# Cross attention over 2048 context rows: heads side by side in row groups of the matrix engine

## What is computed

```python
q = (Q @ Wq.T + bq).reshape(m, -1, H, HD)      # l1x; l2x has no biases on q, k, v and no mask
k = (K @ Wk.T + bk).reshape(m, -1, H, HD)
v = (V @ Wv.T + bv).reshape(m, -1, H, HD)
energy = jnp.einsum('mqhd,mkhd->mhqk', q, k) * SCALE
energy = jnp.where(mask == 0, jnp.float32(-1e+20), energy)
out = jnp.einsum('mhqk,mkhd->mqhd', softmax(energy, axis=3), v)
```

## Time and profile before

| what | before |
|---|---|
| time, median of 3 runs | 623.72 us (621.22 to 623.9) |
| the profiled execution | 620.94 us, span 619.1 us |
| busy: TensorE / its weight loads | 496.6 us (80%) / 379.5 us (61%) |
| busy: DVE / ACT / POOL | 346.1 / 233.6 / 54.0 us |
| chain that ended last | PE 58%, DVE 26%, ACT 7%, issue 4%, DMA 3% |
| mean granted TensorE clock | 0.891 |
| DMA | 42.97 MB, mean 69 GB/s |

### The profile page before, as it was taken

The page is one execution under the profiler, slowest core; times in us unless marked ns, Lnnn a source line. Parts: engine busy times, 40 slices in busy tenths (PEclk is TensorE's granted clock), DMA queues, the critical chain, the costliest instruction groups (busy, mean ns, idle before and its releaser), DMA issues.

```text
span 619.1 us, 9252 instructions
## 1 busy us (share of the span) xinstructions
PE 496.6 (80%) x3712; PEld 379.5 (61%) x3712; DVE 346.1 (56%) x790; ACT 233.6 (38%) x452; POOL 54.0 (9%) x116
## 2 busy tenths in 40 slices
PE   6788659999658706899977677778999999878686
PEld 4656556444538606444446567767888888777685
DVE  5464458771569324867434654346777666643533
ACT  7013305778014202056723314235555555501031
POOL 0400020000022011100021021200000000000000
PEclk9777959999978958599998986989999999987899
DMA  8628100000619784400020000000000000045000
GB/s 292 283 52 167 57 0 1 1 2 2 257 52 371 157 199 178 170 0 1 2 103 1 1 1 1 1 1 1 1 0 1 1 2 1 0 170 238 1 1 5
DMA packets 8005, 42.97 MB, mean 69 GB/s; under 512 B 1050, under 2 KB 4122, under 8 KB 4762
## 3 DMA queue, kind: packets, MB, share of 16 engines
q1 hardware_dynamic: 6811, 33.71, 16.7%
q0 software_dynamic: 1152, 8.68, 3.9%
HBM read 35.69 MB, written 0.08 MB: 58 GB/s over the span
## 4 chain that ended last, share of the span: by engine, by line
PE 58%; DVE 26%; ACT 7%; issue 4%; DMA 3%; POOL 1%; SPq 0%; POOLq 0%; DVEq 0%; ACTq 0%
PE banks L260 53%; PE banks L263 5%; DVE small L2150 3%; ACT probs L2225 3%; DVE peaks L1373 3%; DVE weights_lo L2160 2%; DMA region<-in_tree_f,leaf_no 2%; DVE xn L346 1%; DVE sbq L1609 1%; POOL mv L352 1%; ACT weights_hi L2238 1%; DMA ctxT<-in_ctxT 1%; DVE tB L1889 1%; DVE xnT L365 1%; DVE st L342 1%
## 5 line engine op out<-in xcount | busy, mean ns | idle before, releaser
L1373 DVE TENSOR_REDUCE peaks<-banks 128x1 f32<-128x1024 f32 x64 | 76.7, 1221 | 16.2 <-PE banks L260 16.0
L260 PE MATMUL banks<-identb 128*128 128x128 bf16 x637 | 48.1, 234 | 23.3 <-DMA region<-in_tree_f,leaf_no 15.0
L263 PE MATMUL banks<-p_first,probs 128*128 128x128 f32 x320 | 51.9, 300 | 14.9 <-ACT probs L618 5.1
L260 PEld LDWEIGHTS banks<-identb 128*128 128x128 bf16 x637 | 43.4, 106 | 26.6 <-DMA region<-in_tree_f,leaf_no 15.7
L2238 ACT CAST weights_hi<-banks 128x512 fp32r<-128x512 f32 x64 | 36.0, 588 | 53.8 <-PE banks L263 53.8
L263 PEld LDWEIGHTS banks<-p_first,probs 128*128 128x128 f32 x320 | 40.1, 153 | 26.0 <-ACT probs L618 6.4
L2150 DVE TENSOR_REDUCE small<-banks 128x1 f32<-128x1024 f32 x32 | 39.0, 1218 | 26.8 <-PE banks L260 26.8
L2160 DVE TENSOR_TENSOR weights_lo<-banks,weights_hi 128x512 fp32r<-128x512 f32 x64 | 41.6, 682 | 13.1 <-ACT weights_hi L2238 13.1
L1434 ACT ACTIVATE probs<-banks 128x512 f32<-128x512 f32 x64 | 34.8, 596 | 32.8 <-PE banks L260 31.8
L1434 ACT ACTIVATE probs<-banks,seen 128x512 f32<-128x512 f32 x64 | 40.2, 686 | 11.8 <-PE banks L260 11.8
L260 PE MATMUL banks<-probs,values 128*32 128x256 f32 x512 | 41.7, 395 | 0.5 <-DVE keysT L1394 0.5
(11 more groups left out here) (435 smaller groups left out, 903.2 us busy)
## 6 DMA issues: line engine op xcount, KB each, us to landing
region<-in_w_l2f SPq DMA_DIRECT2D x1, 4096.0 KB, 12.8
region<-in_w_l3f SPq DMA_DIRECT2D x1, 4096.0 KB, 12.0
region<-in_w_b SPq DMA_DIRECT2D x1, 3076.0 KB, 10.3
values<-in_ctx SPq DMA_DIRECT2D x2, 1024.0 KB, 7.7
region<-in_w_l0f SPq DMA_DIRECT2D x1, 2048.0 KB, 21.6
keys_l1x<-shared SPq DMA_DIRECT2D x8, 256.0 KB, 4.0
keys_l2x<-probsT SPq DMA_DIRECT2D x8, 256.0 KB
region<-in_w_l3d SPq DMA_DIRECT2D x1, 2048.0 KB, 15.6
```

The source lines that it names most:

```text
L260: return nc.tensor.matmul(o, lhsT, rhs, start=start, stop=stop)
L263: return nc.tensor.transpose(o, i, ident[0:n, 0:n])
L1373: nc.vector.tensor_reduce(peaks[:, h // 4 % 2, i:i + 1], ps[:, 2 * a:2 * a + 2, :], AX.XY, ALU.max, negate=True).then_inc(VM.sem, VM.now(( ...
```

## The change

- Each head of a quad gets a row group of 32: 8 rows of high, 8 of high, 8 of remainder, then three rows for mask and shift (`ROWS_OF` = 27). The query is `packed`: 128 columns per quad, no spreading.
- `peak(k)` now does one context bank for two heads: two matmuls of 512 columns in neighbouring row groups. DVE reduces 128x1024 to two columns, and a reduce over the four banks follows.
- `scores(u)` does two units (two heads, the same four context tiles): eight matmuls of 27 rows with 128 columns, alternating between two row groups. `weigh(w, half)` waits for the exps of all four heads.
- The query is made in two parts, quad 0 first; the weights' columns are regrouped by ACT copies (`regroup`), the bias comes in by a matmul, the mask's sign as a scale.
- l2x's keys are projected in l1x's lead-in, between its peaks (`early`), copied by ACT twice; POOL makes the remainders; SP stacks them right then. l2x's values move behind l1f's last node product. l2x's lead-in gets `keep(9, 7)` per peak, and the trees of k and v lose their `keep`.
- Stacking takes 48 DMAs of 64 KB per stage. The rows for mask and shift come by four more DMAs. The `w_l0f` load is issued after the mask row.
- The k tree's leaf lies in `probs` and `values_t`.

The core of the diff:

```diff
-            sp.wait_ge(V.sem, V.at((tag, "low", 3)))
+            low = G if tag == "l2x" else V
+            sp.wait_ge(low.sem, low.at((tag, "low", 3)))
+            if tag == "l2x":
+                for g in range(4):
+                    r = slice(32 * g + 24, 32 * g + ROWS_OF)
+                    load("rows_l2x", keys_r["l2x"][r, :, :].bitcast(F32), keys_r["l1x"][r, :, :].bitcast(F32))
             for t in range(4):
                 for part in range(3):
-                    src = (high if part < 2 else keysT[:, :])[32 * t:32 * t + 32, :]
-                    load("keys_" + tag, keys_r[tag][32 * part:32 * part + 32, t, :].bitcast(F32), src)
-                if tag == "l1x" and t:
-                    load("keys_" + tag, keys_r[tag][96:97, t, :].bitcast(F32), keys_r[tag][96:97, 0, :].bitcast(F32))
...
+                    src = high if part < 2 else keysT[:, :]
+                    for g in range(4):
+                        row = 32 * g + 8 * part
+                        load(f"keys_{tag}{t}", keys_r[tag][row:row + 8, t, :].bitcast(F32).rearrange("p (a b) -> p a b", a=2),
+                             src[32 * t + 8 * g:32 * t + 8 * g + 8, :].rearrange("p (a b) -> p a b", a=2))
...
+            sp.wait_ge(V.sem, V.at("mask.row"))
+            sp.wait_ge(A.sem, A.at(("shown", 3)))
+            for g in range(4):
+                load("rows_l1x", keys_r["l1x"][32 * g + 24:32 * g + 25, :, :].bitcast(F32),
+                     bc(keysT[96:97, :], 1, [1, 4, CTX]))
...
             stack_keys(sp, "l1x", shared[:, :])
-            loaded(sp, "keys_l1x")
+            loaded(sp, "keys_l1x3")
             load("node", nodew, dram["node"])
             load("node", nbias, dram["nbias"].partition_broadcast(P))
+            stack_keys(sp, "l2x", wide_high)
+            loaded(sp, "rows_l2x")
             sp.wait_ge(V.sem, V.at("l1x.o"))
             load("w_b", region[:, w_b_at:w_b_at + width(W_B)], dram["w_b"])
             load("w_c", region[:, w_b_at + width(W_B):2 * REG], dram["w_c"])
-            sp.wait_ge(T.sem, T.at(("o", "k")))
-            stack_keys(sp, "l2x", wide_high)
...
+        def key_scalar(act, b):
+
+            act.wait_ge(T.sem, T.at(("l2x", "kp", b)))
+            c = slice(b * BANK, (b + 1) * BANK)
+            nc.scalar.copy(wide_high[:, c].bitcast(F32R), ps[:, KEY_BANKS[b], :])
+            nc.scalar.copy(keysT[:, c], ps[:, KEY_BANKS[b], :]).then_inc(A.sem, A.now(("l2x", "k", b)))
+
+        def low_gpsimd(pool, b):
+
+            pool.wait_ge(A.sem, A.at(("l2x", "k", b)))
+            c = slice(b * BANK, (b + 1) * BANK)
+            nc.gpsimd.tensor_tensor(keysT[:, c], keysT[:, c], wide_high[:, c], ALU.subtract).then_inc(
+                G.sem, G.now(("l2x", "low", b)))
...
+                pe.wait_ge(A.sem, A.at(tag + ".wq"))
                 pe.wait_ge(V.sem, V.at(tag + ".xn.T"))
                 for t in range(4):
-                    m = mm(ps[:, 4, t * P:(t + 1) * P], w("q")[:, t * P:(t + 1) * P], xnT[:, :])
-                m.then_inc(T.sem, T.now(tag + ".q"))
-                loaded(pe, "keys_" + tag)
+                    o = ps[:, 5 if t else 4, t * P:(t + 1) * P]
+                    m = mm(o, at["w_l0x"][:, t * P:(t + 1) * P], xnT[:, :], True, not masked)
+                    if masked:
+                        m = mm(o, bias_rows[:, :], ident[0:4, t:t + 1].broadcast_to([4, P]), False, True)
+                    if t in (0, 3):
+                        m.then_inc(T.sem, T.now((tag + ".q", t // 3)))
...
-                    for b in (2 * a, 2 * a + 1):
-                        m = mm(ps[:, b, :], query_r[0:SHOWN, h * P:(h + 1) * P],
-                               keys[0:SHOWN, h // 4, b * BANK:(b + 1) * BANK])
-                    m.then_inc(PS.sem, PS.now((tag, h, a)))
...
+                    for g in (2 * a, 2 * a + 1):
+                        m = mm(ps[:, g, :], packed[group(g), q * P:(q + 1) * P],
+                               keys[group(g), q, c * BANK:(c + 1) * BANK])
+                    m.then_inc(PS.sem, PS.now((tag, k)))
 
...
-                def score(u):
-
-                    q, t = u // UNITS, u % UNITS
-                    if t == 0:
+                def scores(u):
+
+                    q, c = u // UNITS, u % UNITS // 4
+                    if u % UNITS == 0:
                         pe.wait_ge(VQ.sem, VQ.at((tag, q)))
...
-                    mm(ps[:, 4 + u % 3, :], keys[0:SHOWN, q, t * P:(t + 1) * P],
-                       query_r[0:SHOWN, 4 * q * P:4 * (q + 1) * P]).then_inc(PU.sem, PU.now((tag, u)))
-
-                def weigh(u):
-
-                    q, t = u // UNITS, u % UNITS
-                    if t == 0 and q:
+                    for j in range(4):
+                        t = 4 * c + j
+                        for i in range(2):
+                            g = (u + i) % 4
+                            if j == 0 and u + i >= 3:
+                                pe.wait_ge(AP_.sem, AP_.at((tag, u + i - 3)))
+                            m = mm(ps[:, 4 + (u + i) % 3, j * P:(j + 1) * P], keys[group(g), q, t * P:(t + 1) * P],
+                                   packed[group(g), q * P:(q + 1) * P])
+                            if j == 3:
+                                m.then_inc(PU.sem, PU.now((tag, u + i)))
+
+                def weigh(w, half):
+
+                    q, c = w // 4, w % 4
+                    if c == 0 and q and not half:
                         pe.wait_ge(VO.sem, VO.at((tag, q - 1)))
-                    pe.wait_ge(AP_.sem, AP_.at((tag, u)))
-                    for i in range(2):
-                        j = 2 * (t % 2) + i
-                        v = t * VW + (2 * q + i) * PW
-                        m = mm(ps[32 * j:32 * j + 32, 7, 0:2 * P], values_t[:, v:v + 32],
-                               probs[:, u % 8 // 4, u % 4 * BANK + i * 2 * P:u % 4 * BANK + (i + 1) * 2 * P],
-                               t < 2, t >= KT_N - 2)
-                    m.then_inc(PV.sem, PV.now((tag, u)))
+                    pe.wait_ge(AP_.sem, AP_.at((tag, 4 * w + 3)))
+                    of = probs[:, w % 2, :].rearrange("p (g j n) -> p g j n", g=4, j=4)
+                    for j in (2 * half, 2 * half + 1):
+                        t = 4 * c + j
+                        for i in range(2):
+                            r = 32 * (2 * (t % 2) + i)
+                            v = t * VW + (2 * q + i) * PW
+                            m = mm(ps[r:r + 32, 7, 0:2 * P].rearrange("p (h n) -> p h n", h=2), values_t[:, v:v + 32],
+                                   of[:, 2 * i:2 * i + 2, j, :], t < 2, t >= KT_N - 2)
...
+                early = {0: (key, 0), 1: (value, 0), 2: (value, 1), 3: (key, 1), 4: (key, 2), 5: (value, 2), 6: (key, 3),
+                         7: (value, 3)}
                 for k in range(9):
                     peak(k)
-                    if masked and k:
-                        value(2 * k - 2)
-                        value(2 * k - 1)
+                    if masked and k < 8:
+                        step, b = early[k]
+                        step(b)
+                    elif not masked and k:
+                        keep(9, 7)
                 if masked:
                     pe.wait_ge(A.sem, A.at((tag, "v", 3)))
                 turn(0)
                 peak(9)
-                score(0)
-                score(1)
+                scores(0)
                 peak(10)
                 for v in range(last // 2):
                     q, c = v // 8, v % 8
                     if v < last // 2 - 1:
-                        score(2 * v + 2)
-                        score(2 * v + 3)
+                        scores(2 * v + 2)
                     if c == 6 and q + 1 < QUADS:
                         turn(q + 1)
                     peak(v + LEAD)
-                    weigh(2 * v)
-                    weigh(2 * v + 1)
+                    if v:
+                        weigh((v - 1) // 2, (v - 1) % 2)
                     if v == last // 2 - 2:
-                        pe.wait_ge(VM.sem, VM.at((tag, H - 1, 1)))
+                        pe.wait_ge(VM.sem, VM.at((tag, PEAKS - 1)))
                         for i in range(QUADS - 1):
                             fold(i)
+                weigh(last // 4 - 1, 1)
...
-                loaded(dve, "keys_" + tag)
-                nc.vector.memset(hi[96:128, :], 1.0 if masked else 0.0).then_inc(V.sem, V.now(tag + ".ones"))
...
-                spread(nc.vector, 0).then_inc(V.sem, V.now((tag, "q", 0)))
...
+                for i in range(2):
+                    dve.wait_ge(A.sem, A.at((tag + ".qhi", i)))
+                    o = packed[:, thirds[i]]
+                    nc.vector.scalar_tensor_tensor(o, product(i), sign[:, 0:1], o.bitcast(F32), ALU.mult,
+                                                   ALU.add).then_inc(V.sem, V.now((tag + ".qs", i)))
...
+                    o = packed[:, q * P:(q + 1) * P]
```

(19 more changed lines are left out.)

277 lines of the change are left out of this document (155 added, 122 removed).

## The result

The changed kernel takes 670.93 us (median of 4 runs, 668.33 to 674.88) against 623.55 us before (4 runs on the same chip): a ratio of 1.077, 95% interval 1.071 to 1.084. The forecast was 604 us, so it fell on the wrong side, by more than any rival allowed. The profiled execution of the changed kernel took 669.75 us (span 667.8).

A forecast was written before the change was run, and what follows sets the result against it. TensorE was taken to bound the cross loops' turns. Savings of 3.0 (loops), 3.0 (l2x start), 3.3 (l1x start), 3.0 (trees) and 4.8 (last gather) made 17.1 us off 620.94: 603.8, rounded to 604, range 588 to 624.

The forecast's parts named there:

- Part 1: Peaks in row groups: two 512-column matmuls in different groups overlap, so a pair costs 0.22 us rather than 0.44.
- Part 2: Scores in row groups: eight 128-column matmuls per turn, 256 loads in a stage instead of 64, taken at 0.47 us.
- S: Time of one turn's scores in the cross loops: 0.47 us, outer bounds 0.25 and 0.93.
- Part 3: The cross loops' turn: 1.49 us against 1.68; with the losses counted, 1.5 us saved per stage, 3.0 for both.
- 0.23 left over and 0.57 weighing, which stay: In a loop turn, array-shape changes and waits (0.23 us) and weighing (0.57) were kept at their old length.
- short fp32r matmuls run at fp32's pace: Rival, chance 0.13: fp32r scores of 128 columns take four passes per column, 0.88 us; turn 1.90, kernel 630.0.
- TensorE stays the bound by 0.1: In loop turns with peaks, TensorE's 1.49 us stays above VectorE's own pace of 1.38.
- late turns: The 11 turns without peaks in each stage: 1.42 us against 1.24, losing 2.0 us per stage.
- Part 4: Starts of the cross stages: 3.0 us saved in l2x (bounds 2 and 4.5), 3.3 in l1x (0 and 5.5).
- Cold they may cost 0.5: In l2x's lead-in, the nine `keep` fillers per step fit when warm; cold they may cost 0.5 us.
- Parts 5 and 6: Tree stage: 3.0 us saved (bounds 1 and 4); wait for the last gather: 4.8 saved (bounds 0 and 5.2).
- Part 7: SP's queue: the stacking in more DMAs stays hidden at 16 to 19 us a stack; counted as 0.

The follow-up runs named there:

- the 27-row stream in two groups: Behind the changed kernel's last result, 40 rounds of 512-column fp32r matmuls with 27 rows in two row groups, TensorE alone; the clock held.
- the fillers: Changed kernel with 8 full 128-row bf16 matmuls per turn only in the lead-in and each loop's first six turns: 662.84 us (1 run).
- the halves: Changed kernel with 64-row tiles in place of 27, other head's rows zero: 643.25 us alone, 621.47 with 6 full matmuls in lead-in and first four turns.
- the last kernel: Changed kernel with 64-row tiles, 6 full matmuls from the ninth peak pair to the loop's sixth turn, first two peak pairs moved earlier: 616.42 us, ratio 0.989.
- The streams: Sequences of matmuls on TensorE behind the changed kernel's last result, varying rows, columns and row groups; 27 rows in one group fell to half clock.
- the paced turns: Behind the changed kernel's last result, 16 changed turns each waiting for a short VectorE copy (0.29 to 0.36 us); the clock fell after three turns.
- the run without fillers: Changed kernel with 64-row tiles in place of 27 and no added full matmuls: median 643.25 us, the execution shown 658.17.
- their stream from idle: Behind the changed kernel's last result, 16 turns with 64-row tiles after some 13 us of idle TensorE; the full clock did not come back.

## Why the prediction was wrong

- **Part 1, the pair overlaps: right.** Two 512-column matmuls take 0.45 as a record, and the 27-row stream in two groups ran 80 in 9.36 us, 0.117 each, half the 0.23 of a single one.
- **Part 2, S: right while it applied.** 0.44 against 0.47. In the full-clock turns behind the fillers it is 0.50 (127.73 to 128.23). The loads set it, as rows 5 suggested: 128 rows by 128 columns came every 112 ns (120 from 767.22 to 780.66) with the load path busy 13.40 of 13.40 us, and two groups of 27 rows every 55 (91 in 5.0 us, load path 5.00 of 5.00).
- **Part 3, the turn: the step that failed.** "0.23 left over and 0.57 weighing, which stay" took every duration from rows at a clock of 1.00 and kept that clock for a turn with a different load on the array. 1.49 was right for the work: at full clock the changed turn takes 1.44 behind the fillers, the halves take 1.44, and the last kernel's loops with fillers in six turns take 57.4 and 57.1 us against 57.7 and 59.3 before. But the changed kernel ran at 2.59 and 2.05: what failed is the step from a duration at one clock to a loop at another, 28 us in each stage. The Trainium skill ("TensorE: Matmul & The Clock Gate", Part 1: The HAM clock gate) says that the gate follows how busy TensorE has been; with that rule nothing was to be feared in a loop that TensorE bounds. The trace disagrees: busy 22.00 of 22.00 us at 0.50. The streams and the paced turns above show in its place that the clock also depends on how many rows the matmuls have, and that in a turn of few rows short waits are enough to lose it. No rival priced it. The nearest, that short fp32r matmuls run at fp32's pace, was refuted by the 0.44, and its 630 would have been too low in any case.
- **Part 3, the bound moves.** "TensorE stays the bound by 0.1" at 1.49 against VectorE's 1.38 was right for an ordinary turn: at full clock VectorE waits 0.22 us in it, in the halves' kernel as in the one with fillers at the entry. But where VectorE's maxima are turned or a quad is taken, TensorE waits for it (0.25 us at 126.34 and 0.51 at 132.08 in that kernel), and at the entry it waited too. The sum had no term for what such waits do.
- **Part 3, late turns: too dear.** The halves' late turns take 1.25 us at full clock (154.64 to 159.66 for four), not 1.42, so at full clock the 2.0 us per stage put down for them would not have been lost. In the changed kernel the half clock hid this.
- **Part 4, the starts: wrong, smaller.** From the stage's start to the first score l1x takes 24.5 us (78.51 to 103.00) against 22.2 before, where 3.3 were to be saved. The preparation takes 5.05 (81.43 to 86.48) where 1.9 was forecast, and the lead-in from first peak to first score 16.5 where 14.3 was. The four bias matmuls, costed at nearly nothing, are fp32 with a load each, and all stand ahead of the first peak (order of time, changed kernel):

```profile
82.13 0.79 PE L268 MATMUL banks<-p_first,bias_rows 4*128 4x128 f32 x2
...
83.44 0.35 DVE L1445 SCALAR_TENSOR_TENSOR query_r<-banks,part_sign,query_r 128x128 fp32r<-128x128 f32 x1 [2.16 <-ACT query_r L1496]
...
86.48 0.79 PE L268 MATMUL banks<-keys_l1x,query_r 27*128 27x512 f32 x1
```

  The first quarter of the query is ready at 83.79, and the first peak starts 2.7 us later, behind the other three quarters' products and biases at 0.72 each. In l2x the first score comes 19.9 us after the start (261.58 to 281.43) against 20.1: 0.3 saved in place of 3.0, since each step of nine fillers and a peak pair took 1.79 us at half clock (276.86 to 278.65). "Cold they may cost 0.5" was the right size for one step, and all steps were cold.
- **Parts 5 and 6, trees and the last gather: right, and the exact sum partly luck.** 7.8 us, of which 2.4 come up to the copy behind the third tree (forecast 3.0) and 5.4 between it and the last gather (forecast 4.8): two misses of 0.6 that cancel. VectorE waits 6.26 us for that gather, against 11.41; its median is 6.7 us against the forecast 6.3 and 11.8 before.
- **Part 7, SP: right in its sum.** The stacks took longer than counted (the second lasts from 104.5 to 151), but nothing waited for them.

What stays open: how the changed kernel's clock would behave with VectorE's reduce made shorter, so that TensorE never waits; that wasn't tried. No run puts waits of one length under matmuls of several row counts, so how rows and waits trade off is not known. Nor was it settled why the halves regained the clock by themselves at 142 us in the run without fillers, when neither their stream from idle nor the second loop of the same execution did (0.50 from 270 to 345).

## What to carry to other kernels

Before you pack a matmul into fewer rows of the array, ask what the removed rows were doing for the clock: every duration in a profile holds at the clock of its own stretch, and an edit that empties the array or makes TensorE wait can change it, whether or not TensorE stays busy. If the packed form is wanted, pad it with rows that carry zeros where they cost no time, and bridge the entry of the loop with full matmuls; here that turned a loss of 7.7% into a gain of 1.1%. Read the granted clock by window first whenever a kernel that TensorE bounds gets slower for no visible reason.
